# An image tower of small layers on one core: gate product over 80 rows, image channels ahead of constants, identity products behind the transposes of tokens

## The reference

```python
t = xp @ w_patch + b_patch                      # patches of 16 x 16 x 3
qkv = layernorm(t, g1, beta1) @ w_qkv           # first attention, 12 heads of 64
...
energy = einsum('bhnd,bhmd->bhnm', q, k) * decay    # third attention, 12 heads of 16
out = einsum('bhnm,bhmd->bhnd', energy, v)
gate = sigmoid(x @ Wg1 @ Wg2)                   # Wg1 192 x 16, Wg2 16 x 192
out = layernorm((out * gate) @ Wo, ln_w, ln_b)
```

## Time and profile before

| | us |
|---|---|
| runs | 436.43, 439.99, 438.72 |
| median | 438.72 |
| the profiled execution | 436.5 |
| its span | 434.8 |
| mean granted clock of TensorE in it | 0.978 of full |

### The profile page before, as it was taken

How to read it: one execution, slowest core, us unless ns; L and a number is a source line. 1 busy time by engine, 2 the same in 40 slices (tenths; PEclk the granted TensorE clock), 3 DMA queues, 4 the chain that set the end, 5 groups by cost and what they waited for, 6 DMA issues and landing times.

```text
span 434.8 us, 7607 instructions
## 1 busy us (share of the span) xinstructions
PE 408.7 (94%) x3025; PEld 332.6 (77%) x3025; DVE 238.3 (55%) x721; ACT 168.4 (39%) x272; POOL 48.2 (11%) x105
## 2 busy tenths in 40 slices
PE   7989998998979999999998999999999999998993
PEld 6958887686558767686645689998999898696683
DVE  2367655603169676778355564567558124567423
ACT  1235541623655646363423354345234401711410
POOL 7042010340000000000001300000000201204002
PEclk9999999999899999999999899999999999969899
DMA  8999300000289000000003994034411000000001
GB/s 202 251 215 251 65 2 2 2 0 0 58 230 275 16 1 2 2 0 2 1 2 79 297 242 124 14 119 128 117 18 49 2 0 0 2 4 0 2 2 36
DMA packets 28657, 30.53 MB, mean 70 GB/s; under 512 B 4867, under 2 KB 24073, under 8 KB 28622
## 3 DMA queue, kind: packets, MB, share of 16 engines
q1 hardware_dynamic: 28072, 29.82, 26.8%
q10 hardware_dynamic: 390, 0.22, 0.2%
q0 software_dynamic: 160, 0.01, 0.0%
HBM read 29.63 MB, written 0.39 MB: 69 GB/s over the span
## 4 chain that ended last, share of the span: by engine, by line
PE 82%; DVE 9%; ACT 4%; issue 2%; POOL 2%; DVEq 0%; POOLq 0%; ACTq 0%
PE ps L1371 73%; PE ps L1375 7%; DVE bn L902 1%; PE ps L1383 1%; DVE front L1040 1%; DVE front L1039 1%; ACT front L623 1%; POOL rstd L488 1%; DVE xn L917 1%; ACT front L716 1%; DVE mv L905 1%; DVE front L1033 1%; DVE wide L1243 0%; DVE tok L991 0%; ACT front L680 0%
## 5 line engine op out<-in xcount | busy, mean ns | idle before, releaser
L1371 PE MATMUL ps<-halves 128*128 128x512 f32 x330 | 81.2, 402 | 2.3 <-ACT halves L592 1.8
L1371 PE MATMUL ps<-front 64*64 64x64 f32 (+3 forms) x912 | 71.8, 265 | 3.8 <-ACT front L722 1.4
L1371 PEld LDWEIGHTS ps<-front 64*64 64x64 f32 (+2 forms) x912 | 64.8, 166 | 12.6 <-issue 4.9
L1371 PEld LDWEIGHTS ps<-halves 128*128 128x128 f32 x330 | 61.8, 191 | 15.9 <-issue 2.0
L1371 PE MATMUL ps<-wide,front 128*128 128x192 f32 x432 | 72.0, 327 | 0.0
L1371 PEld LDWEIGHTS ps<-wide,front 128*128 128x128 f32 x432 | 70.4, 190 | 1.0 <-issue 0.5
L668 ACT ACTIVATE front<-ps,colc 128x512 f32<-128x512 f32 x60 | 40.1, 689 | 52.8 <-PE ps L1371 52.7
L1375 PE MATMUL ps<-ident,front 128*128 128x128 f32 (+1 forms) x192 | 28.6, 276 | 4.0 <-ACT front L716 1.7
L1375 PEld LDWEIGHTS ps<-ident,front 128*128 128x128 f32 (+1 forms) x192 | 20.9, 137 | 9.1 <-ACT front L716 2.4
L487 POOL TENSOR_SCALAR rstd<-mv 128x2 f32<-128x2 f32 (+1 forms) x15 | 3.3, 219 | 219.7 <-DVE mv L905 219.7
L1191 DVE SCALAR_TENSOR_TENSOR xn<-ps,small,xn 128x192 f32<-128x192 f32 x28 | 9.7, 410 | 31.3 <-PE ps L1371 31.3
(11 more groups left out here) (257 smaller groups left out, 534.4 us busy)
## 6 DMA issues: line engine op xcount, KB each, us to landing
wide<-in_w SPq DMA_DIRECT2D x8, 576.0 KB, 4.5
wide<-in_w SPq DMA_DIRECT2D x8, 384.0 KB, 5.9
wide<-in_w SPq DMA_DIRECT2D x16, 192.0 KB, 6.3
front<-in_a2w SPq DMA_DIRECT2D x5, 576.0 KB
front<-in_a1w SPq DMA_DIRECT2D x5, 384.0 KB
front<-in_x SPq DMA_DIRECT2D x3, 512.0 KB, 7.5
front<-in_w_qkv SPq DMA_DIRECT2D x2, 576.0 KB, 7.2
front<-in_a1w SPq DMA_DIRECT2D x5, 192.0 KB
```

Source lines behind the costliest of these rows:

```text
L1371: return pe.matmul(o, l, r, start=start, stop=stop)
```

## The change

- On VectorE the block of seven instructions on constants moves behind the three channels. The helper definitions that stood between move with them.
- On TensorE the 14 first identity products become 12, and identity products are added between five turns and their `xT_ready`: 6, 5, 8, 4 and 8, behind turns 1, 3, 4, 5 and 6.
- The gate product reads rows 0 to 79 of `wg2` and `g1T` in place of 64 to 79. GpSimd fills rows 0 to 63 of both with zeros: `wg2` ahead of the fill of `a1w`, `g1T` behind the last expert's first product, with a fifth `pad_made` for which TensorE waits ahead of the gate product.

```diff
--- before.py
+++ after.py
@@ -542,6 +542,7 @@
             pool.wait_ge(s["gu_mm"], NT)
             pool.wait_ge(s["silu_done"], NT)
             pool.wait_ge(s["ln_done"], 3 * NT)
+            link(pool.memset(wg2[0:DB], 0.0))
             tell(pool.memset(a1w[DB:P, :, 1, :], 0.0), "pad_made")
             pool.wait_ge(s["chain_in"], 2)
             pool.dma_start(chE, chS[8:16]).then_inc(s["chE_in"], 16)
@@ -551,6 +552,8 @@
 
             pool.wait_ge(s["h_mm"], NF * EM)
             tell(pool.memset(vbd3, 0.0), "zeros_made")
+            pool.wait_ge(s["h_mm"], NF * (EM + 1))
+            tell(pool.memset(g1T[0:DB], 0.0), "pad_made")
             norm()
 
             pool.wait_ge(s["xT_mm"], 5)
@@ -852,6 +855,65 @@
                 dve.tensor_copy(xq[:, c].rearrange("p w (r q) -> p r w q", r=8),
                                 xr[:, c, :].rearrange("p (r w q) -> p r w q", r=8, w=GRID)).then_inc(s["xq_done"], 1)
 
+            for c in range(C):
+                pixels_in(c)
+                dve.wait_ge(s["xr_T"], 2 * c + 1)
+                dve.tensor_copy(patch_out(c, 0), patch_in(c, 0)).then_inc(s["xpT_dve"], 1)
+
...
             dve.wait_ge(s["consts_made"], 1)
             link(dve.tensor_scalar(par_i[:, :], par_i[:, :], 4, 1, ALU.logical_shift_right, ALU.bitwise_and))
             link(dve.tensor_copy(parity[:, 1:2], par_i[:, :]))
@@ -860,66 +922,6 @@
             link(dve.tensor_copy(pair[:, 1:2], pair_i[:, :]))
             link(dve.tensor_scalar(pair[:, 0:1], pair[:, 1:2], -1.0, 1.0, ALU.mult, ALU.add))
             dve.tensor_scalar(dist[:, :], dist[:, :], 0.0, None, ALU.max).then_inc(s["dist_ready"], 1)
-
-            for c in range(C):
-                pixels_in(c)
-                dve.wait_ge(s["xr_T"], 2 * c + 1)
-                dve.tensor_copy(patch_out(c, 0), patch_in(c, 0)).then_inc(s["xpT_dve"], 1)
-
...
             dve.wait_ge(s["bpatch_in"], 16)
             for j in range(2):
                 dve.wait_ge(s["patch_mm"], j + 1)
@@ -1405,7 +1407,7 @@
                         ins.then_inc(s["patch_mm"], 1)
 
             pe.wait_ge(s["ident_made"], 1)
-            keep_busy(14, 3)
+            keep_busy(12, 3)
             turn_pixels(0)
             keep_busy(6, 3)
             pe.wait_ge(s["wpatch_in"], 16)
@@ -1465,6 +1467,7 @@
 
             keep_busy(9, 3)
             turn_tokens(xn, 1, 1, twice=True)
+            keep_busy(6, 3)
             xT_ready(1)
 
             def split_product(o, w, n, x, turn=0):
@@ -1621,6 +1624,7 @@
                     turn_weights(i + 1)
             pe.wait_ge(s["tok_done"], 4)
             turn_tokens(tok, 3)
+            keep_busy(5, 2)
             xT_ready(3)
             pe.wait_ge(s["wt_act"], 4)
             pe.wait_ge(s["wt_dve"], 4)
@@ -1777,6 +1781,7 @@
             gate_up(3, ((3, 0), (2, 1))).then_inc(s["gu_mm"], 1)
             keep_busy(14, 2)
             turn_tokens(xn, 4, 3, bank=0, twice=True)
+            keep_busy(8, 2)
             xT_ready(4)
 
 
@@ -1825,6 +1830,7 @@
                     down(hT[:, d % 2], w2s[:, d % NSLOT], 4 + 2 * (d % 2), halves=d == EM - 1)
             keep_busy(10, 2)
             turn_tokens(xn, 5, 4, bank=0, twice=True)
+            keep_busy(4, 2)
             xT_ready(5)
 
 
@@ -1844,8 +1850,9 @@
             split_product(ps[:, 1, :], w3x, slice(P, 2 * P), xs).then_inc(s["q3_mm"], 1)
             split_product(ps[0:DB, 2, :], w3x, slice(2 * P, 2 * P + DB), xs).then_inc(s["q3_mm"], 1)
             pe.wait_ge(s["gate1_done"], 1)
+            pe.wait_ge(s["pad_made"], 5)
             for c, (r0, n) in enumerate(CH):
-                ins = mm(ps[0:n, 6 + c, :], wg2[DB:DB + 16, r0:r0 + n], g1T[DB:DB + 16], True, True)
+                ins = mm(ps[0:n, 6 + c, :], wg2[0:DB + 16, r0:r0 + n], g1T[0:DB + 16], True, True)
             ins.then_inc(s["gate3_mm"], 1)
             pe.wait_ge(s["q3_done"], 4)
             for g in range(2):
```

More of the change, by code:

```diff
@@ L853, in pixels_in @@
                                 xr[:, c, :].rearrange("p (r w q) -> p r w q", r=8, w=GRID)).then_inc(s["xq_done"], 1)
[L855 to L862, removed]
             for c in range(C):
@@ L921, in of @@
                 return lambda i: x[:, i, :]
+            dve.wait_ge(s["consts_made"], 1)
+            link(dve.tensor_scalar(par_i[:, :], par_i[:, :], 4, 1, ALU.logical_shift_right, ALU.bitwise_and))
+            link(dve.tensor_copy(parity[:, 1:2], par_i[:, :]))
+            link(dve.tensor_scalar(parity[:, 0:1], parity[:, 1:2], -1.0, 1.0, ALU.mult, ALU.add))
+            link(dve.tensor_scalar(pair_i[:, :], pair_i[:, :], 5, 1, ALU.logical_shift_right, ALU.bitwise_and))
+            link(dve.tensor_copy(pair[:, 1:2], pair_i[:, :]))
+            link(dve.tensor_scalar(pair[:, 0:1], pair[:, 1:2], -1.0, 1.0, ALU.mult, ALU.add))
+            dve.tensor_scalar(dist[:, :], dist[:, :], 0.0, None, ALU.max).then_inc(s["dist_ready"], 1)
             dve.wait_ge(s["bpatch_in"], 16)
```

## The result

The change made the kernel faster. Its first four executions had a median of 430.88 us (430.32 to 432.28) against 438.25 of before, a ratio of 0.9857 with a 95% interval of 0.9814 to 0.9899. Run again beside other kernels, with six executions, it gave 431.29 us and 0.987 (0.9828 to 0.9912). The forecast was 431.8 with a range of 428.5 to 437.0. The profiled execution has a span of 428.6 us, 6.2 less than the earlier trace rows.

The account below looks back on a forecast made before the run. TensorE was taken to set the end almost everywhere, losing time to clock drops and waits. Span 434.8 - 1.8 - 4.3 - 0.8 = 427.9; the 6.9 us gain off the 438.72 median gave 431.8, range 428.5 to 437.0.

Parts of the forecast that it names:

- Start, -1.8: First 20 us: image channels copied ahead of the constants let TensorE start sooner; 1.8 us carried to the first bias addition.
- what is late next is the second channel: At the start: second channel lands at 9.66, copy takes up to 0.85, transposes at 10.56 not 12.33; gain 1.8 us.
- the gain is not carried: Rival on the start: second channel or a small load lands later, or transposes wait on ScalarE; 433.6 us, chance 0.11.
- Identity products, -4.3: Behind five turns: filled waits avoid three clock drops, 4.56 us, less 0.3 us of overruns.
- The cap of 1.16 behind the third turn: Drop there costs up to 1.8 us, but only 1.16 counted: ScalarE waited that long, then its copies set the pace.
- drops move: Rival: shifted work brings a drop at a gap without new products and a late one at the scores; 435.3, chance 0.22.
- Gate product, -0.8: Third attention: gate product over 80 rows, not 16, shortens the narrow stretch before the clock falls; 0.8 of at most 2.5 us.
- most of the stretch is left, and a later drop would hit the value and output products: Third attention: score products keep 32 rows, so the gate gain was taken nearer to nothing, 0.8 us between 0 and 2.5.
- The cost of fills and wait, 0: GpSimd zero fills of wg2 and g1T and TensorE's new wait: covered by idle time; 0.3 us without cover.
- No clock gained: Rival: too few new products, the clock falls as before, also behind the scores; 437.2 us, chance 0.12.
- Slower: Rival: clock already fallen when the new products run, each taking 0.45 us not 0.223; 444 us, chance 0.05.
- new drops stand elsewhere: Sign for the whole kernel: clock drops at new places would make the whole prediction wrong; no size given.

Follow-up runs that it names:

- start_only: Kernel before with only the image channels ahead of the constants on VectorE and 12 identity products for 14: 434.64 us, ratio 0.9953.
- no_ident: Changed kernel without the five added groups of identity products, so start and gate product only: 431.49 us, ratio 0.9888.
- rows32: Kernel before with the 25 identity products ahead of the last turn cut to 32 rows, 128 columns kept: 441.90 us, one execution.
- rows16: Kernel before with the 25 identity products ahead of the last turn cut to 16 rows, 128 columns kept: 443.19 us, one execution.
- rows80: Kernel before with the 25 identity products ahead of the last turn cut to 80 rows, 128 columns kept: 438.71 us, one execution.
- turns128: Kernel before with 25 transposes of the 128-row identity in place of the 25 identity products ahead of the last turn: 440.01 us, one execution.
- gate_only: Kernel before with only the gate product over 80 rows, its two zero fills and its wait: 435.26 us, ratio 0.9958.
- after_again: The changed kernel run again with no edit: 431.29 us over 6 executions, ratio 0.987 to before.
- merged_fill: merged plus seven identity products in a wait of the second attention and four in one of the third: 428.76 us, ratio 0.9818 to before.
- merged: Changed kernel with eight narrow products ahead of the last expert's second product made four over 64 zero-filled rows: 427.77 us, ratio 0.98 to before.

## Why the prediction held, point by point

**The sum and the direction** were right: 6.9 us forecast, 7.4 in the first runs, 5.2 by the medians of the second. Two of its three terms had the wrong size, and the errors cancelled, which is luck. The starting point was off as well: the 438.72 of three executions was a high median, and the 35 and 11 later ones gave 436.4 and 436.5. From 436.5 the forecast gain of 6.9 us would lead to 429.6, and the changed kernel took 431.29 beside it.

**Start, -1.8.** Right in mechanism and size: 2.07 in the pair of profiles, 2.05 or 1.76 by start_only. The first step came a little sooner than forecast (transposes at 6.43, not 6.65). The step "what is late next is the second channel" was right, and the row with 1.64 us of VectorE waiting for in_x shows it. I had taken 0.85 us for that copy; it took 0.69, and the channel landed at 9.46 and not 9.66, which is the difference to 2.07. That the gain is not carried is refuted.

**Identity products, -4.3.** For the pair of profiles the working holds: 1.65 + 1.53 + 1.60 against 1.16 + 1.7 + 1.7. The cap of 1.16 behind the third turn was wrong: the whole drop was won. The 24 records behind that turn took 7.25 us before and 5.59 in the changed kernel, and the lead had grown by 1.65 at the next turn. As a forecast of the median the term failed. It rested on one execution in which the clock fell behind three turns. The other profiles without these products show one such fall (start_only, no_ident), one or two ahead of their own edit (rows32, rows16), two (rows80, turns128) or three (gate_only). Turn by turn, over the eight profiles without them, the clock fell behind the third turn in one only, that of before. It fell behind the fourth in six, and behind the first, which the sum put at nothing, in five. Measured alone the part gave 1.6 us, on top of the others 0.2 to 0.8. None of the six profiles of kernels with the products has a fall behind a turn, so they do what they are for. But part of what they save is lost at the narrow products near 343, as the rival "drops move" had it: four of four profiles against two of eight. How large that part is on the mean can't be told from one profile each.

**Gate product, -0.8.** The mechanism was right and the size was off. The step that failed is to take 0.8 of at most 2.5 us because "most of the stretch is left, and a later drop would hit the value and output products". The later drop came, in four of six profiles, and cost no more there than before: in three of them the value products took 3.62 us, with the 16-row gate 3.55 to 3.98. The scores over 32 rows alone take 3.8 us at the high clock and are over before the clock falls. What made them take 5.0 to 6.4 us was the 16-row product before them. The working had a small slip too: at the high clock 70 score records take 2.8 us (96 in 3.79), not 2.2. Alone the part gave 1.8 us, and its removal from the change costs 3.4 us (0.9948 against 0.987, in two series on two chips), or 3 to 4 us of lost clock (9.0 against 5.7 and 4.5). Not all of that clock is time: TensorE now waits 0.36 and, in after_again, another 0.61 us for VectorE ahead of the value products. The plain reading of the Trainium skill ("TensorE: Matmul & The Clock Gate", part 1), that a busy engine keeps the clock, does not hold in rows16, where TensorE has no idle time and the clock falls.

**The cost of fills and wait, 0.** Right: gate_only and rows16, with the same falls before, reach the gate product 0.03 us apart, and the product takes 2.02 us against 2.12.

**The rivals.** "No clock gained" is refuted by the lost clock, 10.4 us before and 5.7 and 4.5 in the two series of the changed kernel. "Slower" did not occur in the change, and did at one place in merged_fill. "Drops move" occurred in part, and with it a sign by which the prediction called itself wrong as a whole, "new drops stand elsewhere". The profiled fall at 343 stood at a place that the prediction had not named, since it looked only at where the clock had fallen before.

## What to carry to other kernels

Read the clock of many executions before a drop in one profile is priced: each execution lists its granted clock, and its product with the span sorts the times better than any single trace. Look for products of few rows, not only for idle time. Rows filled up with zeros cost TensorE nothing here (2.02 against 2.12 us), and two narrow products that add into one bank can become one. Identity products in a wait must be sized for the high clock and are a loss where the clock has already fallen.

## What the runs showed of the hardware that I had not expected

Products of 16 or 32 rows keep TensorE busy 1.00 and do not hold its clock: 50 records took 7.00 us with 16 rows and 6.45 with 32, where 80 or 128 rows take 5.75. The 16 us that begin with the last of them had a clock of 0.57. Products of 80 rows and of 64 rows (merged) were followed by no such fall. The clock can also fall in the middle of a dense stretch, right behind something narrow, and dense products pay: at 343 us, 31 records at 0.220 us and not at 0.168. The times of one and the same kernel lie 5 us apart, and their lost clocks 5.3 (7.8 and 13.1).
